# A four-layer mixer kernel: the mask folded into one engine's product, the weighting cut in four, and PSUM banks taken over block by block

## The reference

```python
# layer 0 conv (stage L0), layer 1 conv (L1, with a mask), layer 3 conv (L3): "triangle" products
a = (zn @ w_ap + b_ap) * sigmoid(zn @ w_ag + b_ag) * m        # m: the mask, in L1 only
b = (zn @ w_bp + b_bp) * sigmoid(zn @ w_bg + b_bg) * m
k = einsum('bikc,bjkc->bijc', a, b)
out = (layer_norm(k) @ w_z + b_z) * sigmoid(zn @ w_g + b_g)
# layer 0 ffn (F0): 16 experts choose their 8 best positions of each row of 512
probs = softmax(x @ gate_w.T + gate_b, axis=positions); vals, idx = top_k(probs, 8)
pooled = sum(vals * x[idx]); h = gelu(pooled @ weight1); o = h @ weight2; out[idx] += o * vals
# layer 1 ffn (R1), layer 2 ffn (R2): batch norm of x @ W, then a recurrence y = sigmoid(wx_t + y @ V.T)
# layer 2 conv (SC): a scan over rows, row + relu(conv1d(previous row))
# layer 3 ffn (F3): each position goes to the 2 best of 8 experts
```

## Time and profile before

| what | value |
|---|---|
| median of three runs | 615.32 us (614.03 to 616.44) |
| the profiled execution: its time, its span | 615.61 us, 613.8 us |
| mean granted clock of TensorE | 0.842 of full speed |
| busy PE, PE weight load | 455.4 us (74%), 356.4 us (58%) |
| busy DVE, ACT, POOL | 383.7 us (63%), 237.9 us (39%), 249.5 us (41%) |

### The profile page before, as it was taken

How to read it: one execution, slowest core, us unless ns; L and a number is a source line. 1 busy time by engine, 2 the same in 40 slices (tenths; PEclk the granted TensorE clock), 3 DMA queues, 4 the chain that set the end, 5 groups by cost and what they waited for, 6 DMA issues and landing times.

```text
span 613.8 us, 8600 instructions
## 1 busy us (share of the span) xinstructions
PE 455.4 (74%) x3018; PEld 356.4 (58%) x3018; DVE 383.7 (63%) x1148; ACT 237.9 (39%) x573; POOL 249.5 (41%) x325
## 2 busy tenths in 40 slices
PE   3788738798575854699658994879769854926996
PEld 2457634677342843399638994469636743914664
DVE  5796595535868487600792448920579489098885
ACT  1576534301465452457351003547449653200000
POOL 2795485000477078200050000500058478117995
PEclk9999967587789895989858999879859995557999
DMA  9100000000000000000000000000000000000323
GB/s 176 44 2 1 1 1 1 0 2 0 0 2 1 1 1 1 1 2 1 1 1 1 1 1 1 1 1 2 1 1 3 1 0 2 0 0 1 50 38 51
DMA packets 34105, 6.02 MB, mean 10 GB/s; under 512 B 33644, under 2 KB 33772, under 8 KB 34029
## 3 DMA queue, kind: packets, MB, share of 16 engines
q1 hardware_dynamic: 34062, 5.46, 5.1%
HBM read 3.36 MB, written 2.10 MB: 9 GB/s over the span
## 4 chain that ended last, share of the span: by engine, by line
PE 54%; DVE 31%; ACT 6%; issue 3%; POOL 3%; DMA 1%; SPq 1%; DVEq 0%; POOLq 0%
PE psum L1242 6%; DVE moments L290 6%; DVE ab L645 5%; PE psum L1003 5%; PE psum L504 5%; PE psum L384 5%; PE psum L1002 5%; DVE z L298 4%; PE psum L534 4%; PE psum L1415 3%; PE psum L545 3%; PE psum L1024 2%; PE psum L1393 2%; ACT z_t L319 2%; PE psum L1435 2%
## 5 line engine op out<-in xcount | busy, mean ns | idle before, releaser
L330 POOL TENSOR_TENSOR z<-z,stats 128x496 f32<-128x496 f32 (+1 forms) x64 | 67.0, 1047 | 136.6 <-DVE z L298 136.6
L384 PE MATMUL psum<-ident,z 128*128 128x128 f32 x256 | 57.6, 371 | 39.6 <-POOL z L330 38.4
L384 PEld LDWEIGHTS psum<-ident,z 128*128 128x128 f32 x256 | 41.3, 191 | 68.6 <-POOL z L330 48.3
L504 PE MATMUL psum<-wp_L,z_t 64*128 64x320 f32 x384 | 65.0, 477 | 11.1 <-DVE tmp L645 6.2
L319 ACT ACTIVATE z_t<-psum 128x512 f32<-128x512 f32 x56 | 40.1, 721 | 67.3 <-PE psum L384 67.3
L290 DVE BATCH_NORM_STATS2 moments<-x_cols 128x6 f32<-128x64 f32 x448 | 61.9, 210 | 2.1 <-POOL x_cols L716 1.7
L504 PEld LDWEIGHTS psum<-wp_L,z_t 64*128 64x128 f32 x384 | 37.3, 198 | 33.9 <-issue 27.4
L327 POOL MEMSET z<- 128x16 f32 x32 | 4.0, 125 | 128.1 <-DVE z L298 128.1
L1095 ACT ACTIVATE ab<-psum,mv 128x128 f32<-128x128 f32 x112 | 41.3, 369 | 19.9 <-PE psum L1003 9.5
L1003 PE MATMUL psum<-ab,R_vt 128*128 128x128 f32 x224 | 48.8, 302 | 0.0
L1002 PE MATMUL psum<-z_t,wbnt 128*128 128x128 f32 x224 | 46.6, 292 | 0.8 <-DVE wbnt L1148 0.8
(11 more groups left out here) (244 smaller groups left out, 934.7 us busy)
## 6 DMA issues: line engine op xcount, KB each, us to landing
x_cols<-in_x_dram SPq DMA_DIRECT2D x16, 128.0 KB, 2.9
out_dram<-x_cols SPq DMA_DIRECT2D x32, 64.0 KB, 1.9
par<-in_par_dram SPq DMA_DIRECT2D x1, 644.5 KB
w<-in_w_dram SPq DMA_DIRECT2D x1, 264.0 KB
w<-in_w_dram SPq DMA_DIRECT2D x1, 256.0 KB
mask<-in_mask_dram SPq DMA_DIRECT2D x1, 64.0 KB
row<-in_row_dram SPq DMA_DIRECT2D x1, 3.3 KB
w2l<-in_w2l_dram SPq DMA_DIRECT2D x1, 2.0 KB
```

What stands on the lines that cost most here:

```text
L330: pool.tensor_tensor(Z4[:, r, :, 0:c], Z4[:, r, :, 0:c], RSTD[:, q].unsqueeze(3).to_broadcast([N, SQ, G, c]), ALU.mult).then_inc(L.s["z"], 1)
L384: m = pe.transpose(bank(b % 2)[:, k * N:(k + 1) * N], block_of(Z)(4 * b + k), ident[:, :])
L504: m = pe.matmul(bank(slot_bank(s) + h, 2 * 5 * C), ZT[rows, s, :], wp[l][rows, :, :], start=True, stop=True)
```

## The change

**Mask.** In L1, DVE multiplies value, mask and sigmoid in one form of instruction (`scalar_tensor_tensor`, the mask read as one number per partition) straight into `AB`. The mask differs from one group g to the next, so a slot takes four instructions of 64 columns. POOL's masking is gone, and POOL does `gate_bias` and `add_x` in L1 as in L0 and L3.

**Takeover.** F0 and R1 use the banks in the order 6, 7, 2, 3, 4, 5 and wait for six `o_mul` before block 0, seven before block 2 and eight before block 4. R1 has six banks in turn instead of four. F3 begins its routing at block 3 instead of 5.

**Weights and weighting in F0.** PE prepares L1's weights before it waits for the top values, in bank 0 (L3's now in bank 1). WGT is made in four pieces of 512 columns, PE transposes each as it comes, into banks 2 and 3, and DVE copies the prepared weights out two steps earlier.

```diff
-        t1 = stage("L1", "norm weights ones tri", "ab", src=XC, scratch=XR, eps=0, e2=EPS)
+        t1 = stage("L1", "norm weights ones tri", src=XC, scratch=XR, eps=0, e2=EPS)
...
-        f0.banks_free = [(t0.s["o_mul"], t0.at["o_mul"] + S // 4)]
-        r1.banks_free = [(t1.s["o_mul"], t1.at["o_mul"] + S // 4)]
+        f0.outputs_of, r1.outputs_of = t0, t1
...
+        AS_FREED = [6, 7, 2, 3, 4, 5]
+
+        def wait_output_read(pe, L, b):
+
+            T = L.outputs_of
+            if T is not None and b % 2 == 0 and b < 6:
+                pe.wait_ge(T.s["o_mul"], T.at["o_mul"] + S // 4 - 2 + b // 2)
...
-            pe.wait_ge(L.s["ab" if L is t1 else "lin"], L.at["ab" if L is t1 else "lin"] + S)
+            pe.wait_ge(L.s["lin"], L.at["lin"] + S)
...
+        def masked_product(dve, s):
+
+            for g in range(G):
+                w = slice(g * 2 * C, (g + 1) * 2 * C)
+                m = dve.scalar_tensor_tensor(out=to_ab(s)[:, g, :], in0=slot(s)[:, g // 2, g % 2, 2 * C:4 * C],
+                                             scalar=mask[:, g * S + s:g * S + s + 1], in1=SIG[:, s % SLOTS, w],
+                                             op0=ALU.mult, op1=ALU.mult)
+            m.then_inc(t1.s["lin"], 1)
...
                 if L is t1:
-                    if s >= 2:
-                        dve.wait_ge(L.s["ab"], L.at["ab"] + s - 1)
-                    dst = TMP[:, s % 2, 0:2 * GC].rearrange("p (h g w) -> p h g w", h=2, g=2)
+                    masked_product(dve, s)
                 else:
-                    dst = to_ab(s).rearrange("p (h g) w -> p h g w", h=2)
-                dve.tensor_tensor(dst, slot(s)[:, :, :, 2 * C:4 * C], sig, ALU.mult).then_inc(L.s["lin"], 1)
-                if L is t1 and s % 4 == 2 and s > 4:
-                    gate_bias(dve, L, s // 4 - 1)
-                    if s > 8:
-                        add_x(dve, L, s // 4 - 2)
-            if L is t1:
-                gate_bias(dve, L, S // 4 - 1)
-                add_x(dve, L, S // 4 - 2)
-                add_x(dve, L, S // 4 - 1)
+                    dve.tensor_tensor(to_ab(s).rearrange("p (h g) w -> p h g w", h=2), slot(s)[:, :, :, 2 * C:4 * C], sig,
+                                      ALU.mult).then_inc(L.s["lin"], 1)
...
-            if L is t1:
-                m = mask[:, :].rearrange("p (g s) -> p g s", g=G)
-                for s in range(S):
-                    pool.wait_ge(L.s["lin"], L.at["lin"] + s + 1)
-                    pool.tensor_tensor(to_ab(s), TMP[:, s % 2, 0:2 * GC].rearrange("p (g w) -> p g w", g=G),
-                                       m[:, :, s].unsqueeze(2).to_broadcast([N, G, 2 * C]), ALU.mult)\
-                        .then_inc(L.s["ab"], 1)
-            else:
-                pool.wait_ge(L.s["w_dve"], L.at["w_dve"] + TRI_W)
-                for b in range(S // 4):
-                    gate_bias(pool, L, b)
-                    add_x(pool, L, b)
+            pool.wait_ge(L.s["w_dve"], L.at["w_dve"] + TRI_W)
+            for b in range(S // 4):
+                gate_bias(pool, L, b)
+                add_x(pool, L, b)
...
-                    if b == 0:
-                        wait_all(pe, L.banks_free)
+                    wait_output_read(pe, L, b)
                     pe.wait_ge(L.s["zt"], L.at["zt"] + b + 1)
-                    m = pe.matmul(bank(2 + r), gw[:, q, :], ZT[:, 4 * b:4 * b + 4, :], start=(q == 0), stop=(q == 1))
+                    m = pe.matmul(bank(AS_FREED[r]), gw[:, q, :], ZT[:, 4 * b:4 * b + 4, :], start=(q == 0), stop=(q == 1))
...
+            tri_weights_pe(pe, t1)
             pe.wait_ge(L.s["top"], L.at["top"] + 1)
...
-            pe.wait_ge(L.s["w"], L.at["w"] + 1)
             for b in range(SEGI // 4):
+                pe.wait_ge(L.s["w"], L.at["w"] + b + 1)
...
-                    m = pe.transpose(bank(b % 2)[:, k * N:(k + 1) * N], WGT[:, i * N:(i + 1) * N], ident[:, :])
+                    m = pe.transpose(bank(2 + b % 2)[:, k * N:(k + 1) * N], WGT[:, i * N:(i + 1) * N], ident[:, :])
...
-            dve.scalar_tensor_tensor(out=WGT, in0=REPL[:, 0:SEGT], scalar=-2.0 * FAR, in1=PROB, op0=ALU.is_lt, op1=ALU.mult)\
-                .then_inc(L.s["w"], 1)
+            for b in range(SEGI // 4):
+                cols = slice(b * BANK, (b + 1) * BANK)
+                dve.scalar_tensor_tensor(out=WGT[:, cols], in0=REPL[:, cols], scalar=-2.0 * FAR, in1=PROB[:, cols],
+                                         op0=ALU.is_lt, op1=ALU.mult).then_inc(L.s["w"], 1)
...
-            later_weights_dve(dve)
+                    later_weights_dve(dve)
...
-                if b == 0:
-                    wait_all(pe, L.banks_free)
+                wait_output_read(pe, L, b)
                 pe.wait_ge(L.s["zt"], L.at["zt"] + b + 1)
-                if b >= 4:
-                    pe.wait_ge(L.s["wx"], L.at["wx"] + b - 3)
-                pe.matmul(bank(2 + b % 4), W["wraw"][:, :], ZTIME[:, :, 4 * b:4 * b + 4], start=True, stop=True)\
+                if b >= 6:
+                    pe.wait_ge(L.s["wx"], L.at["wx"] + b - 5)
+                pe.matmul(bank(AS_FREED[b % 6]), W["wraw"][:, :], ZTIME[:, :, 4 * b:4 * b + 4], start=True, stop=True)\
...
-                if b == 5:
+                if b == 3:
                     wait_all(pe, L.early_banks_free)
                     for a in range(b - 1):
                         route(a)
-                if b >= 5:
+                if b >= 3:
                     route(b - 1)
...
-        for L, b, col in ((t0, 2, 0), (t1, 2, 0), (t3, 3, 0), (f3, 4, 0), (r1, 5, 0), (r2, 5, GC)):
+        for L, b, col in ((t0, 2, 0), (t1, 0, 0), (t3, 1, 0), (f3, 4, 0), (r1, 5, 0), (r2, 5, GC)):
...
         def later_weights_pe(pe):
-            tri_weights_pe(pe, t1)
             tri_weights_pe(pe, t3)
```

More of the change, by code:

```diff
@@ L848, in f0_act @@
                 act.wait_ge(L.s["lg_ps"], L.at["lg_ps"] + b + 1)
-                act.activation(LOG[:, b * BANK:(b + 1) * BANK], bank(2 + b), ACT.Identity, bias=pcol("gate_b"))\
+                act.activation(LOG[:, b * BANK:(b + 1) * BANK], bank(AS_FREED[b]), ACT.Identity, bias=pcol("gate_b"))\
                     .then_inc(L.s["lg_act"], 1)
@@ L917, in f0_dve @@
                 dve.wait_ge(L.s["wt_ps"], L.at["wt_ps"] + b + 1)
[L918 removed]
+                dve.tensor_copy(WT[:, 4 * b:4 * b + 4, :], bank(2 + b % 2)).then_inc(L.s["wt_dve"], 1)
                 if b == 1:
```

6 lines of the change are left out of this document (3 added, 3 removed).

## The result

The changed kernel takes 593.64 us (median of 4 runs, 589.29 to 594.32), the kernel before 615.88 in the same comparison (the three runs above and a fourth): a ratio of 0.962 (0.959 to 0.965). The forecast of 604.7, range 597 to 611, had the direction right and half the size: 22 us were gained, not 11. The profiled execution of the changed kernel has its own time of 593.35 us and a span of 591.6.

A forecast was written before the change was run, and what follows sets the result against it. The prediction took waits on PE (54%) and DVE (31%) as the bound, neither alone. Its terms, -2.2 - 2.9 - 3.2 - 4.2 + 1.9 = -10.6, took 615.61 to 605.0, or 604.7 us on the median's scale, range 597 to 611.

The forecast's parts named there:

- Term 5: L1's product with the mask on DVE: 32 slots at 1.0 us each, 1.9 us lost.
- I take 0.25: L1's product: a piece of 330 ns less overlap comes every 0.25 us, 1.0 us a slot.
- pieces are cheap: Rival for L1's product: strided write hides behind the next start, 0.20 us a piece, 597.1 us in all; chance 0.17.
- Term 1: First takeover of PSUM banks, L0 to F0: DVE's waits for ACT leave the path, 2.2 us gained.
- rival of a low clock at the takeovers: Clock stays low at the first two takeovers, which gain only 0.6 and 2.0 us; 608.2 us in all; chance 0.18.
- Term 2: F0: L1's weights prepared before the top values fill PE's idle time; 2.9 us gained.
- at the lower clock it sticks out by 1.2: F0: L1's weights take 3.41 us and overrun PE's idle 2.19 us by 1.2 us; gain 2.2.
- the 5.4 us of the upper end: F0's weights and weighting: if PE keeps the upper clock, the weighting's first quarter bounds and 5.4 us are gained.
- Term 3: Second takeover of PSUM banks, L1 to R1, with six banks turning instead of four: 3.2 us gained.
- Term 4: F3's routing after L3: three routes fill PE's idle time before the old first route; 4.2 us gained.
- so 4.2 us idle: F3: of 6.4 us before the first route, two turns of 1.12 us leave PE 4.2 us idle.
- DVE and POOL block each other: Rival in L1: the mask counts as a second SBUF input and waits for POOL; +16, 620.7 us; chance 0.09, shared with full write cost.

The follow-up runs named there:

- fours: The changed kernel, with DVE in L3's product waiting until the sigmoids of four slots are there, then making four products in a row; 608.0 us.
- mask_alone: The kernel before with only the mask part of the change (L1's pieces on DVE, bias and x passes on POOL); 610.28 us.
- weights_late: The changed kernel, with L1's prepared weights behind the top values again, in front of L3's; 597.23 us.
- after_again: The changed kernel as it is, measured and profiled a second time; 594.32 us.
- f0_waits: The changed kernel, with F0's first logits matmul waiting for all eight gate products of L0 again; 596.15 us.
- mask_on_pool_8: The changed kernel with the mask on POOL again, eight TMP buffers instead of two, DVE keeping the bias and x passes; 594.01 us.

## Why the prediction was wrong in size

- **Term 5, the mask on DVE, 1.9 us lost: wrong.** The step that failed is "I take 0.25". The piece's duration was built up rightly from column count, scalar and step (330 ns, measured 318). What was subtracted as overlap was wrong: 0.125 us of a piece overlap, not 0.057 to 0.10. The smaller of those came from products that ACT paced. No row of the trace before shows a strided product at DVE's own pace. The first four products of that stage, 0.449 us apart, give 0.155 and a piece of 0.175, but they follow ACT too, and only `fours` showed that DVE's own pace is nearly the same. Why a piece overlaps by 0.125 and the wide product by 0.155, no run says. With the measured 0.1925 the stage gains 4.95 us. This step is 6.8 of the 11.6 us by which the sum missed the fall of the median. The rival "pieces are cheap" had the mechanism, a strided write that hides, and nearly the size, 0.20 a piece.
- **Term 1, 2.2 us: right,** 2.51 measured. The rival of a low clock at the takeovers fell at both. At the first, PE's matmul of 1.96 us at 87.19 and one of 1.92 at 96.68 ran at the lower level, and the next one behind each took 1.02. Behind each PE soon waited for POOL again (1.65 us at 92.09, 0.47 at 100.88), so neither held up what came after. At the second takeover only the first matmul was slow, 1.85 us at 223.93.
- **Term 2, 2.9 us: right size, wrong about the clock.** 3.97 and 4.34 us in two profiles against the one before. With the 13.69 us of `mask_alone` and the 14.18 of `weights_late` the old order averages 14.2 us, and the twelve profiles with the new order and the early start average 10.9, so 3.3 us is the better figure. The step "at the lower clock it sticks out by 1.2" failed: the weights, right behind the logits, took 2.0 us at the upper level (104.57 to 106.6) and stuck out by nothing. Behind them the clock fell, so the 5.4 us of the upper end weren't reached. The quarters gave nothing in this profile: the whole weighting would have been ready at 112.55 + 2.29 = 114.84, and PE came to it at 114.87. In `after_again` PE came 0.34 us before that time and in `f0_waits` 0.8 us, so they can give a little. No run has them alone.
- **Term 3, 3.2 us: right,** 3.55 measured.
- **Term 4, 4.2 us: right mechanism, too small,** 5.10 measured. The failed step is "so 4.2 us idle". The two turns in the gap were counted at 1.12 us each; between routes a turn costs 0.75, since it overlaps its neighbours (from the first route to F3's reduction 16.80 us with four turns, 15.31 before with two), and the first route starts 0.90 us behind the start of a turn. 7.49 - 0.90 - 1.49 = 5.10.
- **"DVE and POOL block each other": fell,** no piece over 329 ns.
- **What stays open.** The five terms make 20.1 us in this pair of profiles; the medians fell by 22.2 and 21.0. The stretches that vary by themselves (start to a, e-f, g-h) follow the granted clock and can carry 1 to 2 us. Over the changed kernels g-h averages about 228.4 us, in the two profiles with all takeovers old 230.1 and 233.0. Whether the change makes the clock steadier or this is chance, two profiles don't settle.

## What to carry to other kernels

A chain of small instructions is priced by the time from one start to the next, not by duration. Take that from a row where the inputs are known to lie ready, and compare it with the pace of the engine that delivers them first; if the two agree, the row doesn't show the engine's own pace, and it takes a run that holds the engine back until its inputs lie ready. Before moving work off an engine that is waited for, look at the buffers in between: here six more of them were worth nearly as much as moving the mask (4.8 and 5.1 us of stage). And cut two traces at the same instructions: many stretches repeat to 0.01 us where whole times scatter by 5.

No run beat the changed kernel with the same result. DVE's pieces need 0.77 us a slot and ACT 0.55, so at most 32 x 0.22 = 7 us are left in that stage; `mask_on_pool_8` took as long as the changed kernel.
